# A twelve-stage decoder on one core: the talking-heads attention loads its rows and weights earlier, and the plain attentions run their first batch in another order

## What is computed

```
q, k, v = x Wq, x Wk, x Wv;  q, k normalized per head
scores  = q . [mem_k ; k] * 10                 16 heads, 128 x 132
scores  = mixed over the 16 heads by W_pre, causal
scores  = the 64 largest of each row kept, softmax
weights = mixed over the 16 heads by W_post
out     = (weights . [mem_v ; v]) * head_scale * sigmoid(x Wg + bg), times Wo
x       = layernorm(x + out)
```

## Time and profile before

| | us |
|---|---|
| median of 3 runs | 1441.05 (1440.38 to 1443.08) |
| profiled execution | 1447.14 |
| its span | 1445.4 |

### The profile page before, as it was taken

The page is one execution under the profiler, slowest core; times in us unless marked ns, Lnnn a source line. Parts: engine busy times, 40 slices in busy tenths (PEclk is TensorE's granted clock), DMA queues, the critical chain, the costliest instruction groups (busy, mean ns, idle before and its releaser), DMA issues. The chain is left out here.

```text
span 1445.4 us, 18406 instructions
## 1 busy us (share of the span) xinstructions
PE 943.6 (65%) x6190; PEld 610.1 (42%) x6190; DVE 1015.2 (70%) x2541; ACT 627.9 (43%) x1329; POOL 123.2 (9%) x261
## 2 busy tenths in 40 slices
PE   4864757555884204455978636999778526967977
PEld 2532333333553103345945313666445223534644
DVE  4868989835554899874448574999578596957833
ACT  3646666622432404443126425655046302634632
POOL 0120000000000000000120120000011021120100
PEclk9975555557986557667989857999679757988968
DMA  5000000001334001112000000000000000000000
GB/s 190 2 1 0 1 1 1 1 1 44 91 90 150 1 0 61 47 44 59 1 1 2 1 1 0 1 1 1 0 1 1 1 0 1 2 1 1 2 1 15
DMA packets 25997, 29.51 MB, mean 20 GB/s; under 512 B 689, under 2 KB 22577, under 8 KB 24882
## 3 DMA queue, kind: packets, MB, share of 16 engines
q1 hardware_dynamic: 25906, 28.35, 6.2%
HBM read 18.91 MB, written 9.44 MB: 20 GB/s over the span
## 5 line engine op out<-in xcount | busy, mean ns | idle before, releaser
L1750 DVE TENSOR_TENSOR_SCAN l2a_hs<-l2a_decay,l2a_b_ps 128x512 f32<-128x512 f32 x64 | 78.0, 1221 | 14.3 <-ACT l2a_decay L1680 6.1
L1605 PEld LDWEIGHTS l2a_b_ps<-l2a_diag,l2a_uT 128*128 128x128 f32 x512 | 64.0, 191 | 39.3 <-issue 38.0
L1605 PE MATMUL l2a_b_ps<-l2a_diag,l2a_uT 128*128 128x128 f32 x512 | 69.9, 280 | 2.0 <-DVE l2a_hs L1750 1.7
L2170 PE MATMUL l1w_mem_ps<-l1w_rows,l1w_post 128*128 128x64 f32 x16 | 4.6, 381 | 96.9 <-DVE l1w_rows L2313 96.9
L1613 PE MATMUL l2a_acc_ps<-l2a_hc,pack 128*128 128x512 f32 x128 | 65.5, 595 | 1.0 <-DVE l2a_hc L1761 1.0
L2286 DVE MATCH_REPLACE8 l1w_minus<-l1w_low,l1w_minus 128x129 f32<-128x129 f32 (+39 forms) x264 | 64.9, 283 | 0.0
L2280 DVE MAX8 l1w_low<-l1w_minus 128x8 f32<-128x129 f32 (+37 forms) x332 | 60.1, 278 | 0.8 <-DVE l1w_minus L2266 0.5
L2198 ACT ACTIVATE l1w_score<-l1w_mix_ps 128x264 f32<-128x264 f32 (+7 forms) x29 | 12.0, 451 | 111.7 <-DVE l1w_rows L2313 92.5
L2160 PE MATMUL l1w_mix_ps<-l1w_rows,l1w_pre 128*128 128x264 f32 (+7 forms) x58 | 30.9, 707 | 45.4 <-DMA l1w_rows<-scores_dram 37.7
L1680 ACT ACTIVATE l2a_decay<-l2a_dt,pack 128x1016 f32<-128x1016 f32 x32 | 36.4, 1141 | 45.4 <-DVE l2a_hs L1750 45.4
L917 ACT ACTIVATE l0x_prob<-l0x_dist,l0x_last_mx 128x128 f32<-128x128 f32 x128 | 38.3, 387 | 21.5 <-DVE l0x_last_mx L1039 21.5
(11 more groups left out here) (586 smaller groups left out, 2720.1 us busy)
## 6 DMA issues: line engine op xcount, KB each, us to landing
scores_dram<-l1p_dots SPq DMA_DIRECT2D x8, 1056.0 KB, 6.8
l1w_rows<-scores_dram SPq DMA_DIRECT2D x8, 1056.0 KB, 5.1
pack<-in_pack SPq DMA_DIRECT2D x1, 697.5 KB, 9.5
pack<-in_pack SPq DMA_DIRECT2D x2, 321.5 KB, 6.6
pack<-in_pack SPq DMA_DIRECT2D x1, 612.0 KB, 11.5
pack<-in_pack SPq DMA_DIRECT2D x1, 576.0 KB, 10.4
pack<-in_pack SPq DMA_DIRECT2D x1, 514.0 KB, 8.0
x_tok<-in_x SPq DMA_DIRECT2D x1, 512.0 KB, 4.2
```

Source lines behind the costliest of these rows:

```text
L1605: mm = nc.tensor.matmul(bx_ps(n)[:, j * S:(j + 1) * S], uT[:, c, b, :], diag[:, s % 2, b, :], start=True, stop=True)
L1750: nc.vector.tensor_tensor_scan(hs[:, n % 2, :], decay[:, k % 2, batches, :].rearrange("p b t -> p (b t)"), bx_ps(n), 0.0, ALU.mult, ALU.ad ...
```

## The change

Talking heads:

- `dots` becomes two tiles used in turn; a batch's copies wait only for the stores of the batch before the last.
- SP stores a batch in two transfers, the 16 queries of the first block (7) first, the other 112 after. When the first store has landed it loads this batch's rows of the first block, and when the second has landed those of the second and third block (three transfers on 16 partitions each). These rows are complete after the last batch, and `mixed_weights` loads only blocks four to eight. The wait for the last store is no longer a step of its own: SP's list ends with the two last loads.
- SP loads wg and wo right behind wq, wk and wv, into memory that no later stage reads again (columns of the weights of the first layer, and pdiff). It loads mem_v and mem_w at the end of `mixed_weights`' list, mem_v ahead of the wait for the memory weights' store, mem_w behind it. `mixed_output` has no transfers of its own; the gates wait for wg, the scaling of wo for wo, the outputs for mem_v and mem_w.
- The quantizing of the later weights moves from the start of `mixed_weights` into `mixed_scores`, on DVE before it waits for the memory keys' transpose.
- ACT copies v after the first fill's copy and not before it. DVE copies the second fill before it scales q. DVE's loop is written out for every batch.

Plain attentions:

- PE no longer waits for `consts_set` before the first projection (ACT still does before it writes v).
- In `score`, the wait for `copy_qk` moves behind the four mask matmuls.
- Except in `l3x`, DVE does in the first step maximum(0, 0) before copy_qk(1).

```diff
@@ attention, PE
                 def score(b):
-                    pe.wait_ge(qk_set, b + 1)
                     after(pe, diff_set, 2 * b)
...
                             nc.tensor.matmul(bank(g), cm.ident_bf[:], bcast_mid(bias_mask, HH), start=True, stop=False)
+                    pe.wait_ge(qk_set, b + 1)
...
-                pe.wait_ge(consts_set, 2)
                 project_qk(0)
@@ attention, DVE
-                    if inside(now + 2):
+                    if inside(now + 2) and (now >= 0 or prefix):
                         copy_qk(now + 2)
...
                         maximum(now + 1, 0)
+                    if now < 0 and not prefix:
+                        copy_qk(now + 2)
@@ mixed_attention
+class LoadedAhead:
+    def __init__(self, cm, sc):
+        self.blocks = [sc.sb(f"rows{n}", [128, ROWS_K, J]) for n in range(ROW_BUFS)]
+        self.loaded_rows = [sc.sem(f"loaded_rows{k}") for k in range(BLOCKS_K)]
+        self.rows_count = [16 * B if k in ORDER_K[0:ROW_BUFS] else 16 for k in range(BLOCKS_K)]
+        self.wg, self.wo = cm.early, cm.pdiff
...
+        spare = self.blocks[(BLOCKS_K - ROW_BUFS) % ROW_BUFS][:].rearrange("p i j -> p (i j)")
+        self.mem_w = spare[:, 0:B * S].rearrange("p (b i) -> p b i", b=B)
+        self.mem_v = spare[:, B * S:B * S + H * E1 // 2]
@@ mixed_scores, SP
-                with sp.Fori(0, B) as b:
+                sp.dma_start(ahead.wg, cm.A["l1a_wg"]).then_inc(ahead.wg_in, 16)
+                sp.dma_start(ahead.wo, cm.A["l1a_wo"]).then_inc(ahead.wo_in, 16)
+                def load_rows(b, n):
+                    k = ORDER_K[n]
+                    r = slice(ROWS_K * k, ROWS_K * (k + 1))
+                    sp.dma_start(ahead.blocks[n][b * H:(b + 1) * H, :, :], scores_dram[b, :, r, :]) \
+                        .then_inc(ahead.loaded_rows[k], 16)
+                for b in range(B):
+                    by_query = scores_dram[b].rearrange("g i j -> i g j")
                     sp.wait_ge(dots_act, 3 * b + 3)
                     sp.wait_ge(dots_dve, 3 * b + 3)
-                    sp.dma_start(scores_dram[b].rearrange("g i j -> i g j"), dots[:]).then_inc(stored, 16)
-                sp.wait_ge(stored, 16 * B)
+                    sp.dma_start(by_query[first], dots[b % 2][first, :, :]).then_inc(first_stored, 16)
+                    sp.dma_start(by_query[others], dots[b % 2][others, :, :]).then_inc(stored, 16)
+                    sp.wait_ge(first_stored, 16 * (b + 1))
+                    load_rows(b, 0)
+                    sp.wait_ge(stored, 16 * (b + 1))
+                    for n in range(1, ROW_BUFS):
+                        load_rows(b, n)
@@ mixed_scores, ACT
-                        act.wait_ge(v_mm, b + 1)
-                        nc.scalar.activation(v_all[:, b, :], v_ps[:], ACT.Copy).then_inc(v_set, 1)
-                        after(act, stored, 16 * b)
+                        after(act, first_stored, 16 * (b - 1))
+                        after(act, stored, 16 * (b - 1))
...
+                            if f == 0:
+                                act.wait_ge(v_mm, b + 1)
+                                nc.scalar.activation(v_all[:, b, :], v_ps[:], ACT.Copy).then_inc(v_set, 1)
@@ mixed_scores, DVE
+                gated.dve_quantize(nc, dve, cm)
                 dve.wait_ge(mem_mm, 1)
...
-                        nc.vector.tensor_tensor(qn[:], heads(q_ps[:]), bcast_last(norm[:, 0, :], E1),
-                                                ALU.mult).then_inc(normed, 1)
                     if cur:
                         copy_dots(b, 1)
                     if nxt:
+                        nc.vector.tensor_tensor(qn[:], heads(q_ps[:]), bcast_last(norm[:, 0, :], E1),
+                                                ALU.mult).then_inc(normed, 1)
                         nc.vector.tensor_tensor(kn[:], heads(k_ps[:]), bcast_last(norm[:, 1, :], E1),
@@ mixed_weights, SP
-                for n, k in enumerate(ORDER_K):
+                for n in range(ROW_BUFS, BLOCKS_K):
...
                 sp.dma_start(mem_dram, mem_w[:]).then_inc(mem_stored, 16)
+                for part in range(2):
+                    p = slice(64 * part, 64 * part + 64)
+                    sp.dma_start(ahead.mem_v[p, :], cm.A["l1a_mv"][:, part * 512:part * 512 + 512]).then_inc(ahead.mem_v_in, 16)
                 sp.wait_ge(mem_stored, 16)
+                for part in range(2):
+                    p = slice(64 * part, 64 * part + 64)
+                    sp.dma_start(ahead.mem_w[p, :, :], mem_dram.rearrange("(b h) m i -> (h m) b i", b=B)) \
+                        .then_inc(ahead.mem_w_in, 16)
@@ mixed_weights, DVE
-                gated.dve_quantize(nc, dve, cm)
@@ mixed_output, PE
-                pe.wait_ge(w_in, 64)
+                pe.wait_ge(ahead.wg_in, 16)
...
                 gates(0)
-                pe.wait_ge(mem_in, 32)
+                pe.wait_ge(ahead.mem_v_in, 32)
+                pe.wait_ge(ahead.mem_w_in, 32)
```

More of the change, by code:

```diff
@@ L2029, in iteration @@
                     if cur:
-                        after(dve, stored, 16 * b)
+                        after(dve, first_stored, 16 * (b - 1))
+                        after(dve, stored, 16 * (b - 1))
                         copy_dots(b, 0)
@@ L2044, in iteration @@
                         copy_dots(b, 2)
-                steps(dve, iteration)
+                for b in range(-1, B):
+                    iteration(b, b + 1 < B, b >= 0)
 def block_width(k):
@@ L2085, in dve_quantize, with mixed_weights @@
         dve.wait_ge(self.step, 7)
-def mixed_weights(nc, cm, scores_dram, mem_dram, mixed):
+def mixed_weights(nc, cm, scores_dram, mem_dram, mixed, ahead):
     with Scope(nc, "l1w") as sc:
@@ L2095, in mixed_weights @@
                  for odd in range(2)]
-        blocks = [sc.sb(f"rows{n}", [128, ROWS_K, J]) for n in range(ROW_BUFS)]
+        blocks, loaded_rows, rows_count = ahead.blocks, ahead.loaded_rows, ahead.rows_count
         minus = sc.sb("minus", [128, ROWS_K * J])
```

63 lines of the change are left out of this document (26 added, 37 removed).

## The result

The changed kernel takes 1407.98 us (median of 4 runs, 1407.16 to 1409.12) against 1440.72 (4 runs, 1439.19 to 1443.08) before: a ratio of 0.9766, 95% interval 0.9748 to 0.9785, 32.7 us less. The forecast was 34.7 less. Measured again later beside the kernel before it was 1405.04 against 1446.93: 0.972, 0.9698 to 0.9741, 41.9 less. The two intervals don't meet, though both kernels are the same: the kernel before is not one time but a band (1439 to 1451 over all its runs), and a kernel's difference from it holds to several microseconds only. The profiled execution of before (1447.14) was 6.1 over the median of its own group, but an ordinary one beside the later runs; that of after took 1407.94, its median. The spans differ by 39.3.

A forecast was written before the change was run, and what follows sets the result against it. No engine was busy over 70%, so time was taken as a sum of blocks between barriers, each with its own limit. Savings 16.5 + 4.5 + 2.0 + 3.5 + 8.2 = 34.7 from the median 1441.05 gave 1406.4 us, range 1397 to 1418.

The forecast's parts named there:

- Attentions: Five plain attentions: earlier start, masks without a wait and earlier first maximum shorten the first batches; 16.5 us saved.
- Loop: Score loop: later v copy and DVE's new order gain 0.9 a batch in five low-clock periods; 4.5 us saved.
- Last batch: Last score batch: with two dots tiles the second fill starts after 0.65 and not 2.70; 2.0 us saved.
- Tail: From the last score copy to the first mix: 8.7 us and not 12.16; 3.5 us saved.
- 0.2 to wake SP: In the tail: SP needs 0.2 us after the last copy, then 0.4 for the first store.
- Output stage: Gates start at once after ACT's last copy and outputs follow without waiting for mem_w; 8.2 us saved, 6.7 at the slow bound.
- Quantizing: Moved from mixed_weights to mixed_scores: hidden under a wait in both places; 0 us.
- the later batches catch up: Rival, attentions: later batches keep their own spacing, so only the starts count; 10 us less gain, 1416.4; chance 0.14.
- late transfers: Rival: small transfers land late, tail gains nothing and mem_w takes the slow bound; 1411.3 us; chance 0.12.
- the store chain: Rival, score loop: SP's stores and loads set the period if landings reach 11 us; 1453 at 16; chance 0.02.
- The clock: Rival: shorter PE idle keeps the clock up, loop gains 8.8, 1402.1 us, or it shifts elsewhere; chance 0.11.

The follow-up runs named there:

- loop_mix: Changed kernel with only DVE's scaling of q put back ahead of the second dots copy, ACT still copying v late: 1410.1 us, ratio 0.9745.
- att_all: Kernel before with all three plain-attention edits alone: 1416.1 us, ratio 0.9799.
- att_start: Kernel before with the plain-attention edits except DVE's reordering: 1430.7 us, ratio 0.9886.
- one_buf: Changed kernel with one dots tile, copies waiting for both stores of the batch before: 1414.0 us, ratio 0.9789.
- tail_m: Changed kernel, rows loaded behind the next batch's stores, last batch's small store first and big one last, its landing awaited in the next stage: 1401.9 us, 0.9685.
- out_loads_back: Changed kernel with the loads of wg, wo, mem_v and mem_w issued again at the start of the output stage: 1413.4 us, ratio 0.9767.
- quant_back: Changed kernel with the quantizing back in the weights' stage, behind DVE's masks: 1407.6 us, ratio 0.9742.
- both_orders: Changed kernel with the edits of both tail_m and loop_mix: 1405.8 us, ratio 0.9733.

## Why the prediction was right, and where it was not

The time (1406.4 forecast, 1408.0 measured, 1405.0 the second time) and the sign hold. Term by term, from the first pair of profiles and in brackets from the second:

- *Attentions* 16.5: measured 19.0 (22.9), and 27.7 alone. The mechanism is as told: masks without a wait, table load exposed, second scores at 10.0 for 10.6, later batches at the same distances. Two sizes were off, with opposite signs: "half of the products (1.05) lets maximum(0, 0) start" is wrong, since the first maximum waits for all of them (2.09 at a granted 0.50, or 1.14 at 1.00); and I priced PE at the low clock (a granted 0.50), while in the first profile it still stood at the full one when the block began (granted 1.00 from 719.3 to 720.0, projections of 0.46 for 0.77) and so did the masks at first (1.36 for 1.89, at 0.70). In the second profile l1x began at a granted 0.50 (717.0 to 719.8), and the products had 0.80 (1.37 for 2.09). l3a gave 5.8 for 3.7, l3x 3.9 for 2.3, l2x 1.2 (3.4) for 3.5.
- *Loop* 4.5: 3.85 (3.68), but not as told. "Then the new order: gap 0.77 as before, then q, k and the third copy in a row" rests on DVE being in the way with q, which costs 0.22, not 1.2. The kernel's order makes the full-clock period 0.3 to 0.8 longer, where I had 0, and gains 0.2 to 0.6 in the low ones, where I had 0.9; `loop_mix` has both advantages. 3.0 of the 3.85 appear in kernels whose loop is unedited (`att_all`, `att_start`), so that this number came near its forecast by luck.
- *Last batch* 2.0: 2.4 (1.8), shown by `one_buf`.
- *Tail* 3.5: 1.7 (1.9), the one mis-sized by half. Of the 1.8 that are missing in the first profile, 0.8 are the step "0.2 to wake SP": SP's list for a batch takes 9.4 (435.19 to 444.63), while the last copies of the last two batches end 8.5 apart (435.11, 443.62), so that SP stored 1.0 after the last copy. In the second profile the list was done in time, SP stored 0.47 after the copy, and the tail was 9.65; so the list explains the difference between the two, not all of the miss. The other terms are the landing of the big store (7.3 and 7.0 from issue to the next load, for 6.8) and 0.4 between SP's last issue (453.10) and DVE's masks (453.54), which I had at nothing. The rows themselves were there, as told; `tail_m` takes that list apart, waits no longer for the big store, and gets 2.1 back. The store and the load on 16 partitions landed in 3.6 (the whole store in 6.8); no run separates in this the number of partitions from the queue.
- *Output stage* 8.2: 8.9 (8.1), of which 1.8 to 2.0 is lost in l1x, which I didn't have. Two errors partly cancel in it: the gates took 2.02 and not 3.71, and `mem_w` was waited for (0.92, 1.11) where I had no wait.
- *Quantizing* 0: 0, in both places.

The terms add up to 35.9 of the 39.3 between the first two spans, and to 38.4 of the 43.4 between the second two. That their sum is so near the forecast of 34.7 is in part luck: the attentions' term is 2.5 too small, those of tail and loop are 2.4 too large together, and nothing was forecast for the untouched blocks.

By rivals: "the later batches catch up" fell (`att_all`); "late transfers" holds for half of the tail; "the store chain" never came near, since SP's list of 9.4 leaves 2.8 of a period of 12.2. "The clock" is what the sum missed. l3f, without an edit, took 41.2, 43.1, 44.5 or 46.3 in these profiles, at granted clocks of 0.83, 0.82, 0.77 and 0.76; l2x with all its edits took 76.5 or 78.7 and l1x 80.5 or 82.5. The changed kernel is among those with the shortest l3f, with `out_loads_back`, `tail_m` and `quant_back`. What decides this level for a block isn't settled: the time differs between kernels that are the same up to the block (l0a, where only the program behind it differs, 76.2 to 77.7 in ten profiles with the edited order, 78.75 in one) and no run changed the clock alone.

## What to carry over

Price a block by its waits, and then give the clock a term of its own: here blocks that no edit touched moved with it by as much as an edit was worth (l3f took 41.2 at a granted 0.83 and 46.3 at 0.76), so shorter by 5 us in one stage may be 0 in the median. And compare two stretches only at the same granted clock, or the clock's share is taken for the edit's, as in the loop. When work is put on a queueing engine's list (here SP's), add up the list for the shortest batch and not for the usual one. Before a reordering is paid for with a new wait, try its halves alone.

## What was unexpected of the hardware

- In l1x four matmuls of 32 rows each, one on each quarter of the rows, let none of their results go early: DVE's wait ends with the last of them, 2.09 after the start of the first at a granted clock of 0.50 (from 756.26 in the kernel before, 730.94 in the changed one) and 1.14 at 1.00 (from 764.83 and 739.97).
- A store of 132 KB on 16 partitions lands in 3.6, while the one of 256 KB on 128 partitions takes 2.0. The two differ in more than their partitions (the first has a store of 924 KB right behind it), so the cause stays open.
- l3f's PE was busy for 38.6 and 33.6 us with the same work, at granted clocks of 0.76 (`both_orders`) and 0.83 (the changed kernel).
